# Two table tiles in each one-hot instruction, and 25 quads of steps picked by TensorE, each over 5 blocks

## The reference

```python
h = relu(layernorm(x))
feat = relu(h @ W_pool + b_pool)
w = edge_weight / max(segment_sum(edge_weight, dst), eps)[dst]
neigh = segment_max(feat[src] * w[:, None], dst)          # 0 where a node has no edge
rst = h @ W1_self + neigh @ W1_neigh + b1
g = relu(rst / max(norm(rst), eps))
neigh2 = segment_sum(g[src] * w[:, None], dst) / max(deg, 1)
out = x + relu(g @ W2_self + neigh2 @ W2_neigh + b2)
```

## Time and profile before

| | |
|---|---|
| median of 3 runs | 4113.24 us |
| the profiled execution | 4112.68 us |
| its span (first to last instruction) | 4110.8 us |
| busy: POOL, DVE, PE, ACT | 3076.6, 2820.1, 2576.0, 1352.4 us |
| mean granted TensorE clock | 0.779 |
| gathers of phase 0 and of phase 1 (L447) | 1451 and 1511 |
| one-hot instructions (L769) | 1862 |

### The profile page before, as it was taken

One profiled execution on the slowest core, in us unless ns is written; L12 is line 12 of the kernel. 1 busy time (PEld: TensorE's weight loads), 2 busy tenths in 40 slices (PEclk: granted clock), 3 DMA queues, 4 the chain that ended last, 5 costly groups with the idle time before them and its releaser, 6 DMA issues. The chain is left out here.

```text
span 4110.8 us, 30816 instructions
## 1 busy us (share of the span) xinstructions
PE 2576.0 (63%) x7403; PEld 1201.8 (29%) x7403; DVE 2820.1 (69%) x6223; ACT 1352.4 (33%) x3994; POOL 3076.6 (75%) x3262
## 2 busy tenths in 40 slices
PE   4133342222378777774667777777777777779856
PEld 4032232222123222221422222222222222224534
DVE  6477797877667776775567777767776777677424
ACT  5333443333333333332533233323332233323320
POOL 7777777777777777776767777777777777777766
PEclk8555555555599999997579899999998989989755
DMA  6233333334433333333433333333333333333335
GB/s 201 89 113 106 105 120 125 125 127 129 130 104 117 107 111 112 105 109 103 102 94 106 114 107 106 117 106 104 117 107 106 114 107 109 114 104 104 114 110 149
DMA packets 206026, 468.02 MB, mean 114 GB/s; under 512 B 57650, under 2 KB 123188, under 8 KB 181012
## 3 DMA queue, kind: packets, MB, share of 16 engines
q0 software_dynamic: 104000, 213.25, 18.5%
q1 hardware_dynamic: 101844, 252.80, 16.8%
HBM read 240.76 MB, written 225.06 MB: 113 GB/s over the span
## 5 line engine op out<-in xcount | busy, mean ns | idle before, releaser
L447 POOL DMA_INDIRECT G<-h_tab,SRC x1511 | 1425.7, 944 | 471.8 <-issue 420.0
L447 POOL DMA_INDIRECT G<-feat_tab,SRC x1451 | 1375.8, 948 | 442.2 <-issue 393.1
L769 DVE TENSOR_SCALAR CP<-pH,kc 128x512 f32<-128x512 f32 x1862 | 1388.4, 746 | 38.6 <-PE pM L925 36.5
L546 ACT ACTIVATE pT<-G,EW 128x128 f32<-128x128 f32 x1522 | 553.8, 369 | 1205.1 <-DMA G<-h_tab,SRC 615.3
L546 ACT ACTIVATE pM<-G,EW 128x128 f32<-128x128 f32 x1440 | 512.2, 367 | 1238.0 <-DMA G<-feat_tab,SRC 593.4
L925 PE MATMUL pM<-CP,A 128*128 128x512 f32 x1372 | 693.5, 654 | 229.8 <-DVE CP L769 229.8
L925 PE MATMUL pC<-CP,A 128*128 128x512 f32 x1176 | 632.7, 695 | 174.0 <-DVE CP L769 174.0
L901 PE MATMUL pH<-CP 128*128 128x98 bf16 x1563 | 144.6, 281 | 603.8 <-DVE CP L727 603.8
L715 DVE SCALAR_TENSOR_TENSOR S<-S,M,pT 128x128 f32<-128x128 f32 x782 | 267.1, 342 | 354.6 <-ACT pT L546 348.0
L712 DVE SCALAR_TENSOR_TENSOR S<-S,C,pT 128x128 f32<-128x128 f32 x782 | 269.7, 345 | 334.3 <-ACT pT L546 320.7
L925 PEld LDWEIGHTS pM<-CP,A 128*128 128x128 f32 x1372 | 235.2, 200 | 674.9 <-DVE CP L769 559.5
(11 more groups left out here) (134 smaller groups left out, 1814.9 us busy)
## 6 DMA issues: line engine op xcount, KB each, us to landing
scan<-S SPq DMA_DIRECT2D x97, 1032.0 KB, 4.1
scan<-S SPq DMA_DIRECT2D x97, 1024.0 KB, 4.0
G<-h_tab,SRC POOLq DMA_INDIRECT x1511
G<-feat_tab,SRC POOLq DMA_INDIRECT x1451
feat_tab<-F SPq DMA_DIRECT2D x24, 256.0 KB, 2.4
h_tab<-A SPq DMA_DIRECT2D x24, 256.0 KB, 2.6
U<-in_x SPq DMA_DIRECT2D x24, 256.0 KB, 3.7
out<-F SPq DMA_DIRECT2D x24, 256.0 KB, 2.6
```

The source lines that it names most:

```text
L447: pool.indirect_dma_start(out=dst, out_offset=None, in_=table, in_offset=bass.IndirectOffsetOnAxis(ap=idx, axis=0)).then_inc(s, 16)
L546: act.activation(scaled(t), v, ACT.Copy, scale=EW[:, t:t + 1]).then_inc(s_mul, 1)
L769: dve.tensor_scalar(OH[:, k % 4, :], pH[:, :], kc[:, j:j + 1], None, ALU.is_equal).then_inc(s_o2, 1)
```

## The change

The quads are spread over 5 blocks instead of 7, so that there are 8 in phase 0 (blocks 54 to 93) and 17 in phase 1 (blocks 0 to 84). One VectorE instruction writes the one-hots of two tiles: a `tensor_tensor` over 128 x 2 x 512, where `pH` is repeated for both tiles and `kc` gives one column for each. `OH` has the same size as before, now two buffers of two tiles. TensorE waits once for two tiles and signals once behind both. There are 49 such pairs in a quad. The steps of the quads, their `TAKEN` and `READ` steps, and the first step of the own rows (from step 1360 to step 1296, one group in 10 steps instead of 8) follow from `QUADS` and `QB`.

```diff
-QB = 7
-QUADS = [(0, 54 + QB * i) for i in range(6)] + [(1, QB * i) for i in range(13)]
+QB = 5
+QUADS = [(0, 54 + QB * i) for i in range(8)] + [(1, QB * i) for i in range(17)]
 QN = len(QUADS)
+NJ = NT // 2
...
-PICKS = {(phase, T * b + j * T * QB // NT): [] for phase, b in QUADS for j in range(NT)}
+PICKS = {(phase, T * b + j * T * QB // NJ): [] for phase, b in QUADS for j in range(NJ)}
...
-        OH = CP[:, 8 * P:24 * P].rearrange("p (k n) -> p k n", k=4)
+        OH = CP[:, 8 * P:24 * P].rearrange("p (k j n) -> p k j n", k=2, j=2)
...
-                        sp.wait_ge(s_o2, (v - 2) * NT + 1)
+                        sp.wait_ge(s_o2, (v - 2) * NJ + 1)
...
-                    act.wait_ge(s_od, (u + 1) * NT)
+                    act.wait_ge(s_od, (u + 1) * NJ)
...
-                if k >= 4:
-                    dve.wait_ge(s_od, k - 3)
-                dve.tensor_scalar(OH[:, k % 4, :], pH[:, :], kc[:, j:j + 1], None,
+                if k >= 2:
+                    dve.wait_ge(s_od, k - 1)
+                dve.tensor_tensor(OH[:, k % 2, :, :], pH[:, :].unsqueeze(1).to_broadcast([P, 2, 4 * P]),
+                                  kc[:, 2 * j:2 * j + 2].unsqueeze(2).to_broadcast([P, 2, 4 * P]),
                                   ALU.is_equal).then_inc(s_o2, 1)
...
                     pe.wait_ge(s_o2, k + 1)
-                    pe.matmul(picked(u), table_tile(phase, j), OH[:, k % 4, :], start=(j == 0),
-                              stop=(j == NT - 1)).then_inc(s_od, 1)
+                    pe.matmul(picked(u), table_tile(phase, 2 * j), OH[:, k % 2, 0, :], start=(j == 0), stop=False)
+                    pe.matmul(picked(u), table_tile(phase, 2 * j + 1), OH[:, k % 2, 1, :], start=False,
+                              stop=(j == NJ - 1)).then_inc(s_od, 1)
```

More of the change, by code:

```diff
@@ L42, in quad_mul @@
     return QUADS[u][0] * TS + quad_steps(u)[-1] + 1
-PICKS = {(phase, T * b + j * T * QB // NT): [] for phase, b in QUADS for j in range(NT)}
+PICKS = {(phase, T * b + j * T * QB // NJ): [] for phase, b in QUADS for j in range(NJ)}
 for u, (phase, b) in enumerate(QUADS):
-    for j in range(NT):
-        PICKS[phase, T * b + j * T * QB // NT].append((u, j))
+    for j in range(NJ):
+        PICKS[phase, T * b + j * T * QB // NJ].append((u, j))
 STARTS = {pb: u for u, pb in enumerate(QUADS)}
@@ L761, in pick @@
             def pick(u, j):
-                k = u * NT + j
+                k = u * NJ + j
                 if j == 0:
@@ L915, in picks @@
                 for u, j in PICKS.get((phase, t), ()):
-                    k = u * NT + j
-                    if u == 0 and j % LT == 0 and j <= K:
-                        pe.wait_ge(s_ft[j // LT], 16)
+                    k = u * NJ + j
+                    if u == 0 and 2 * j % LT == 0 and 2 * j <= K:
+                        pe.wait_ge(s_ft[2 * j // LT], 16)
                     if j == 0 and u == 0:
```

## The result

The changed kernel took 4083.32 us (median, 4082.60 to 4083.57, four runs) against 4113.11 us (4112.89 to 4114.64, four runs): a ratio of 0.9926, 95% interval 0.9909 to 0.9944, so some 0.7% faster. The forecast was 4084 us. The profiled execution took 4083.49 us (before 4112.68) with a span of 4081.8 us (before 4110.8).

What follows compares the result with a forecast made beforehand. The prediction took POOL's gather list, 1.248 us a step, as the bound: 4112.7 - 30.0 for 24 steps + 1 for the last quad = 4083.7, with 0.6 for the median 4084 us; forecast 4082 to 4088, range 4080 to 4096.

Steps and rivals of the forecast that it cites:

- POOL is the pace: Both edge phases: POOL's gather list sets the time, 1.248 us a step; 24 more steps without a gather save 30.0 us.
- The pair costs 1.22 us and 1.135 from start to start: DVE's new one-hot instruction, sized from the histograms' rows; a quad then takes 77.1 of 94.9 us, 81%.
- the two ways of counting: DVE's work per quad: 77.1 us counted from start to start, or 88.1 us with full durations, against 94.9 us.
- The new pattern does not slow POOL: POOL's gathers beside the new instruction's repeated inputs: no slowdown, priced at 0.
- PE keeps up, at a higher clock: PE in ordinary quads: 84.9 us (phase 1) or 89.1 (phase 0) of 94.9, needing mean clocks above 0.895 and 0.94.
- that rival: PE bounds every quad at clock 0.83: 225 us more, about 4309 us; chance 0.05 slower than before, 0.03 mild form.
- The last quad: Picks beside own rows: 16 us of PE lag against 19 that POOL bears; cost 1 us, bounds 0 and 8.
- Its last link: ACT's copy of the picked bank, 4 steps behind the last pair: ACT stands 0 to 3 us, which the slots cover.
- DVE waits for PE over 38 us in the last quad: A sign to look for in the last quad's trace: DVE's waits for PE total over 38 us.
- The ends of the phases: Tails of both phases become ordinary gathers without picks beside them: between -2 and +2 us, taken as 0.
- the sum of 4083.7 us: Whole execution: the profiled 4112.7 us, less 30.0 for gathers left out, plus 1 for the last quad.
- the rule of the cover: DVE's pick time rises from 1229 to 1390 us in all, yet costs nothing only because POOL covers it.

## Why the prediction was right, point by point

The prediction was for a chip like that of the first profile, and the changed kernel was timed there. Its steps:

**POOL is the pace, 1.248 us a step.** Right. Phase 0 gave 9.9 us for 8 gathers. The rows of POOL's waits before gathers, both phases together (total us, times, longest piece), show where a wait was:

```profile
POOL G L448 <- issue: 780.2, 2560, 0.3
...
POOL G L448 <- ACT pM L547: 73.3, 237, 1.4
...
POOL G L448 <- ACT pT L547: 42.7, 140, 0.3
```

In the rows for ACT pM 236 pieces of 0.305 us make 72.0 us, and one of 1.37 us the rest. It is the only long wait of POOL for ACT in the edge phases.

**The pair costs 1.22 us and 1.135 from start to start.** Right, from the histograms' rows. By form, and in order of time in a dense run:

```profile
L770 DVE TENSOR_TENSOR CP<-pH,kc 128x1024 f32<-128x1024 f32 x1225 | 1494.5, 1220 | 94.0 <-PE pM L928 55.4 <-PE pC L928 22.2 <-issue 0.2
```

```profile
2798.80 1.23 DVE L770 TENSOR_TENSOR CP<-pH,kc 128x1024 f32<-128x1024 f32 x1
2799.94 0.72 DVE L716 SCALAR_TENSOR_TENSOR S<-S,M,pT 128x128 f32<-128x128 f32 x2
2800.58 1.22 DVE L770 TENSOR_TENSOR CP<-pH,kc 128x1024 f32<-128x1024 f32 x1
2801.71 0.34 DVE L716 SCALAR_TENSOR_TENSOR S<-S,M,pT 128x128 f32<-128x128 f32 x1
```

1220 ns; the next start 1.14 and 1.13 us after it. The prediction called this a difference from the Trainium skill (VectorE: DVE Perf Modes, The DRAIN you can't avoid), by which the next instruction does not start until the pipe is empty. It took that rule as wider than it is: the same section adds that an instruction that is not held starts earlier. The start times here, which lie before the end of the record, agree with the addition. The choice between the two ways of counting changed no time, since DVE stayed below POOL by both.

**The new pattern does not slow POOL.** Right: 944 ns a gather of phase 1, as before, and 1.248 us from one to the next, beside the pairs.

**PE keeps up, at a higher clock.** Right, and this was the condition that mattered. 0.895 and 0.94 were needed, 0.99 and 0.98 were granted, from 0.92 and 0.94 before. The fuller PE had the higher clock here; a stretch of 10 us inside a quad, columns as above:

```profile
2610.00:2620.00 10.00, 8.93 (x22) 3.56 (x20) 8.42 (x15) 3.26 (x9) 7.56 (x9) 1.00 0.32 92
```

With one of the clocks of the earlier trace rows, 0.83, the prediction put the time some 225 us above the forecast (an estimate, which no run tests); that rival had 0.05. One figure beside it is off, without effect: before the change PE's share in a quad of phase 0 was, by the prediction's own terms, 90.8 of 134.8 us, 67% and not 70%.

**The last quad.** Right in its size, for the stated reason. Changed kernel, order of time:

```profile
3696.05 0.60 PE L984 MATMUL pR<-ident,A 128*128 128x128 f32 x4
...
3701.74 1.23 DVE L770 TENSOR_TENSOR CP<-pH,kc 128x1024 f32<-128x1024 f32 x1 [3.62 <-PE pM L928]
...
3706.95 1.22 DVE L770 TENSOR_TENSOR CP<-pH,kc 128x1024 f32<-128x1024 f32 x1
...
3707.88 0.94 POOL L448 DMA_INDIRECT G<-h_tab,SRC  x1 [0.30 <-issue]
...
3708.55 1.50 DVE L716 SCALAR_TENSOR_TENSOR S<-S,M,pT 128x128 f32<-128x128 f32 x4
...
3710.32 0.60 ACT L552 ACTIVATE CP<-pM 128x512 f32<-128x512 f32 x1 [5.38 <-PE pM L928]
...
3711.45 0.94 POOL L448 DMA_INDIRECT G<-h_tab,SRC  x1 [1.37 <-ACT pM L547]
```

At 3707.88 POOL issues the 1315th gather of phase 1, step 1378, and DVE begins step 1360 at 3708.55: a lead of 18 where 17 to 20 was forecast, and 13 steps or 16 us of lag. The gap of 1.37 us instead of 0.30 is the whole price, 1.07 us where 1 was taken. That 1 and 1.07 meet so closely is partly luck, since the prediction's bounds were 0 and 8. Its last link was priced too low: ACT stood 5.38 us at the copy of the picked bank, not 0 to 3. PE had a group of own rows from 3696.05 to 3699.7 us, DVE waited 3.62 us for a product behind it, and so its last pairs came late. The copy also stands 5 steps behind the last pair (step 83 against 78), not 4 as the prediction has it.

**DVE waits for PE over 38 us in the last quad.** Wrong. The groups by line from 3600 to 3720 us:

```profile
L770 DVE TENSOR_TENSOR CP<-pH,kc 128x1024 f32<-128x1024 f32 x48 | 58.6, 1221 | 26.3 <-PE pM L928 25.7
```

25.7 us lie there. The waits of the pairs for PE in the whole run are two rows (total us, times, longest):

```profile
DVE CP L770 <- PE pM L928: 55.4, 85, 5.5
...
DVE CP L770 <- PE pC L928: 22.2, 62, 1.4
```

So 52 of the 77.6 us are waits in the other 24 quads, for which the prediction gave no figure. They cost nothing, since none reached POOL.

**The ends of the phases**, -2 to +2 us and taken as 0, were -1.3 and +2.1. With the -1.0 up to the first gather they nearly cancel (-0.2 us), and so the sum of 4083.7 us met the profiled execution of 4083.49. That much of the agreement is luck.

**What the prediction did not cover.** It said that the pairs cost nothing "only because POOL covers it", and priced the cover's loss as a pair that is too long. On the other chips it was lost in another way: signals reach DVE late in spells, POOL then waits, and each pair costs some 0.2 to 0.7 us. That the change is slower there (1.028) agrees with the rule of the cover. Of the rivals only that of the low clock comes near: it named a mean under 0.88 in phase 1, and 0.87 was granted there. But PE was busy only 77% of that window, so PE is not the bound there as that rival has it.

**Left open.** No experiment met the situation of the first chip. So for it the account above rests on the trace alone, and it stays untested what each part of the change gives alone, whether the own rows begun later would give the 1.07 us back, and whether 27 quads would gain or 32 would make PE the bound. On the other chips 9 and 3 quads (4886 and 4865 us) beat both kernels; on the first chip the changed kernel is the fastest that was measured.

## What to carry to other kernels

Find the engine that never rests, price a step on it, and check every other engine for its share of that step from start to start and at its slowest likely clock: here 30.0 us were forecast and 28.8 came between the gathers. Size a new instruction from one that repeats its inputs in the same way. Work that is free because another engine covers it is free only where that engine is the pace, so time such a change on more than one chip and occasion before it is adopted: here the first chip gave 0.993 for this kernel, and four others 1.028 to 1.031 for it or for near relatives. When two traces of one program differ, look first at whether both hold the same number of events.

## What the runs showed of the hardware

- One program took 4113 us in one situation and 4985 to 5011 us on six chips in another, at nearly equal durations of its instructions (944 and 946 ns a gather, 1220 and 1222 ns a pair). The difference lies in late starts, which come in spells; whether the chip is the reason is not shown.
- In the second situation many starts follow a signal that is late: 778 of the 1003.6 us that DVE stood before pairs lie after the end of the product that the pair needed, and none in pieces of over 0.5 us in the first.
- The granted TensorE clock rose with the work: a mean of 0.92 before and 0.99 after in phase 1, with PE busy 76% and 92%. More work on PE was partly paid by a faster PE.
